# Moving the 16-bit low parts of the slot rows from GpSimd to VectorE in an early-fusion mixture-of-experts block

## What is computed

```python
h = patch_embed(x); h = concat([h, txt], axis=1)                 # 32 x 333 x 192
h = h + sdconv(layernorm(h))      # per token: softmax over 9 taps, weighted window of 9 values
xf = layernorm(h).reshape(-1, D)
scores, idx = top_k(xf @ Wg, 2); weights = softmax(scores)
for k in range(2):                # capacity int(1.2 * N / 8) tokens per expert and choice
    xg = xpad[buf]                # gather the tokens of each expert
    h1 = einsum('ecd,edh->ech', xg, W1)
    ye = einsum('ech,ehd->ecd', h1[..., :H] * silu(h1[..., H:]), W2)
    out = out.at[buf].add(w_buf * ye)
h = h + out
```

## Time and profile before

| what | value |
|---|---|
| median of 3 runs | 1479.6 us (1479.3 to 1480.26) |
| the profiled execution's own time | 1478.12 us |
| its span, first to last instruction | 1476.2 us |
| stage 1, up to the first matmul of stage 2 | 808.5 us |
| busy in the span: PE, DVE, ACT, POOL | 85%, 67%, 30%, 48% |

### The profile page before, as it was taken

How to read it: one execution, slowest core, us unless ns; L and a number is a source line. 1 busy time by engine, 2 the same in 40 slices (tenths; PEclk the granted TensorE clock), 3 DMA queues, 4 the chain that set the end, 5 groups by cost and what they waited for, 6 DMA issues and landing times. The chain is left out here.

```text
span 1476.2 us, 23362 instructions
## 1 busy us (share of the span) xinstructions
PE 1249.6 (85%) x8476; PEld 991.4 (67%) x8476; DVE 991.2 (67%) x1924; ACT 449.7 (30%) x949; POOL 715.1 (48%) x545
## 2 busy tenths in 40 slices
PE   6969888988989798843640999999999999999994
PEld 6757666777767576533330787787777778877873
DVE  4107959999999999997841565656564655656552
ACT  2011222223232222212031443434442434344331
POOL 1000221766666665746376345545556255455455
PEclk9989998999989898765755999999999999999997
DMA  9795563655656554623024455464656365554533
GB/s 328 299 357 154 134 175 87 183 150 158 180 161 171 153 139 110 155 74 100 23 69 122 84 79 89 62 111 55 103 61 106 58 100 64 91 78 61 71 46 36
DMA packets 224279, 178.52 MB, mean 121 GB/s; under 512 B 128872, under 2 KB 208006, under 8 KB 224160
## 3 DMA queue, kind: packets, MB, share of 16 engines
q1 hardware_dynamic: 176896, 117.16, 32.7%
q0 software_dynamic: 37248, 36.15, 16.1%
q10 hardware_dynamic: 10016, 23.66, 4.3%
HBM read 69.22 MB, written 89.23 MB: 107 GB/s over the span
## 5 line engine op out<-in xcount | busy, mean ns | idle before, releaser
L1127 POOL DMA_INDIRECT out<-yb,meta x200 | 329.4, 1647 | 323.2 <-DVE yb L1184 252.2
L1216 DVE TENSOR_TENSOR hidden<-silu,bankU 128x320 f32<-128x320 f32 x320 | 155.2, 487 | 198.0 <-PE bankU L1249 172.7
L902 PE MATMUL bankK<-normedT,conv_w 128*128 128x333 f32 x864 | 278.7, 471 | 0.0
L85 POOL DMA_INDIRECT expert_inputs<-slot_rows,slots x176 | 230.0, 1307 | 78.4 <-issue 55.0
L1156 ACT ACTIVATE silu<-bankG 128x320 f32<-128x320 f32 x320 | 139.8, 437 | 379.7 <-PE bankG L1249 358.4
L902 PEld LDWEIGHTS bankK<-normedT,conv_w 128*128 128x128 f32 x864 | 169.5, 202 | 78.0 <-issue 13.1
L1262 PE MATMUL bankY<-w_high,hidden_high 128*128 128x192 f16 x800 | 197.2, 246 | 0.0
L1263 PE MATMUL bankY<-w_low,hidden_high 128*128 128x192 f16 x800 | 197.2, 246 | 0.0
L1264 PE MATMUL bankY<-w_high,hidden_low 128*128 128x192 f16 x800 | 197.2, 246 | 0.0
L652 DVE TENSOR_TENSOR prod<-window_values,kb 128x960 f32<-128x960 f32 (+1 forms) x135 | 168.3, 1255 | 3.6
L670 DVE TENSOR_TENSOR hidden_group<-hidden_group,prod 128x960 f32<-128x960 f32 (+1 forms) x135 | 169.1, 1253 | 0.5
(11 more groups left out here) (131 smaller groups left out, 2212.7 us busy)
## 6 DMA issues: line engine op xcount, KB each, us to landing
patches<-in_x SPq DMA_DIRECT2D x16, 1536.0 KB, 8.6
token_rows<-rowbuf SPq DMA_DIRECT2D x32, 492.0 KB
expert_inputs<-prod ACTq DMA_DIRECT2D x8, 1470.0 KB, 15.0
window_values<-token_rows SPq DMA_DIRECT2D x32, 264.0 KB, 5.5
hidden_group<-token_rows SPq DMA_DIRECT2D x32, 264.0 KB, 7.1
expert_inputs<-prod ACTq DMA_DIRECT2D x8, 980.0 KB, 16.6
window_values<-token_rows SPq DMA_DIRECT2D x32, 192.0 KB, 5.7
kb<-token_rows SPq DMA_DIRECT2D x32, 148.5 KB, 4.7
```

The costliest lines, as they stand in the source:

```text
L85: nc.gpsimd.indirect_dma_start(out=xslots[:, :], out_offset=bass.IndirectOffsetOnAxis(ap=idx[g % 2][:, k, r:r + 1], axis=0), in_=xrow[g % ...
L902: mm = T_.matmul(bankK[(u + t) % 2][:, 0:L], conv_w[:, t // 2, k, :], qT[u][:, t, k:k + L], start=(k == 0), stop=(k == K - 1))
L1127: nc.gpsimd.indirect_dma_start(out=out[:, :], out_offset=bass.IndirectOffsetOnAxis(ap=meta[t % NMETA][:, c, 0:1], axis=0), in_=yb[v][:, c, ...
L1216: V.tensor_tensor(hf[j % 2][:, m * HALF:(m + 1) * HALF], sg[m][:, :], bankU[m][:, 0:HALF], ALU.mult).then_inc(prod_done, 1)
```

## The change

`low_parts` is also defined for DVE, with the same two subtractions (L682 and L683 in the changed kernel, for L375 and L376). DVE does the low parts of both slices of groups 0 to 5 and of slice 0 of group 6: 13 of 16 calls. Slice 1 of a group is done one iteration later than POOL did it, in front of slice 0 of the next group, right behind the norm of the iteration's second pair. Its last two calls, (5, 1) and (6, 0), stand behind the loop. POOL keeps (6, 1), (7, 0) and (7, 1), and its scatters now wait for DVE.

```diff
 # POOL
                 for it in range(NG):
                     pair_norm(2 * it + 1)
-                    if it > 1:
-                        low_parts(it - 2, 0)
                     if it > 2:
                         scatter(it - 3, 0)
...
                     if it > 2:
                         scatter(it - 3, 1)
-                    if it > 1:
-                        low_parts(it - 2, 1)
                     if it:
                         slice_norm(it - 1, 0)
-                low_parts(NG - 2, 0)
                 scatter(NG - 3, 0)
 # DVE
+                def low_parts(g, s):
+                    ss, x16 = slice(*SLICES[s]), xrow16[g % 2]
+                    dve.wait_ge(xh_ready, NSL * g + s + 1)
+                    V.tensor_tensor(x16[:, ss, LOB:LOA], xn[:, ss, 128:D], x16[:, ss, 128:D], ALU.subtract)
+                    V.tensor_tensor(x16[:, ss, LOA:META], xn[:, ss, 0:128], x16[:, ss, 0:128], ALU.subtract)\
+                        .then_inc(xl_ready, 1)
...
                     attend(p, 0)
                     if it:
                         norm(p + 1)
+                    if it > 2:
+                        low_parts(it - 3, 1)
                     if it > 1:
+                        low_parts(it - 2, 0)
                         part(2)
...
                 g, h = NG - 1, NG - 2
+                low_parts(NG - 3, 1)
+                low_parts(NG - 2, 0)
                 part(2 * NSL * K)
```

## The result

| what | before | changed |
|---|---|---|
| median, first comparison | 1479.45 us (4 runs) | 1490.07 us (4 runs, 1488.19 to 1491.62) |
| ratio to before | | 1.0065, 95% interval 1.0044 to 1.0085 |
| the same two kernels again (run z1) | 1478.92 us (17 runs) | 1492.32 us (6 runs), ratio 1.0089, 1.0072 to 1.0106 |
| profiled execution's own time | 1478.12 us | 1490.28 us |
| its span | 1476.2 us | 1488.5 us |

The change costs 10.6 us by the medians and 12.2 between the profiled executions; 8.2 were forecast. All but 0.2 of the 12.2 lies in stage 1, whose end came 12.0 later.

A forecast was written before the change was run, and what follows sets the result against it. DVE, busy 75.73 of 80.20 us an iteration, was taken as the bound. The terms 12.5 - 5.1 - 1.5 + 0.3 + 2.0 gave +8.2 us on 1479.6, so 1487.8 us, own range 1484.0 to 1492.4.

The forecast's parts named there:

- the first rival: The port between POOL and DVE stays contested, L636 stays long and 5.1 us come back: 1493 us, chance 0.15.
- Added to DVE: Iterations 3 to 7: four subtractions lengthen each by 2.5 us, +12.5 us in all, bounds +11.1 and +14.1.
- Clash removed: Iterations 3 to 7: without POOL's low parts (L375, L376), DVE's L636 falls back to 1.40 us, -5.1 us in all.
- A DMA wait covered: L632's wait for the window DMA in three iterations vanishes as DVE arrives 2.5 us later: -1.5 us, bound 0.
- The other waits: DVE's waits on the text DMA and PE start from L636 or later and move along: 0.
- Iteration 2: Only slice 0's subtractions, 1.35 us against 1.20 given back at L636: +0.3 us, between 0 and 0.8.
- The tail: Behind the loop: DVE waits 4.0 us for high parts, POOL's slice norm starts 1.1 later: +2.0 us, -0.1 to +3.0.
- The port stays contested: L636 stays long beside scatters, and DVE's subtractions can hold up POOL's pair norm: +13.3 us, 1493, chance 0.15.
- A wash: All low ends, and the tail costs nothing: +1 to +3 us, about 1481 us, chance 0.12.
- Faster: A loop over POOL, ACT and PE back to DVE sets the period; subtractions fill waits: 1471 us, chance 0.07.

The follow-up runs named there:

- z2: The changed kernel with each pair of DVE's subtractions done twice, the second time over the same data: 1510.43 us, 1.0207.
- y3: Kernel before, POOL's slice 0 low parts held until slice 1's windows are through, tail slice norm (6, 1) before low parts and scatters: 1485.63 us, 0.9995.
- x4: The changed kernel without the two subtractions in DVE's 13 calls, those low parts left zero, waits and semaphore raises kept: 1483.28 us, 0.9983.
- x3: The kernel before with POOL's low parts of slice 0 moved behind the first seven scatters, nothing moved to DVE: 1488.24 us, 1.0036.
- z4: The kernel before with only low parts (0, 0) of iteration 2 on DVE, all others on POOL: 1479.45 us, 1.0003.
- x1: The changed kernel with its two tail calls, (5, 1) and (6, 0), back on POOL as before: 1495.96 us, 1.0080.
- the filler: A quarter of PE's patch matmuls put ahead of the third set of transposes: changed kernel 1485.82 us, 1.0013; kernel before 1479.08 us, 0.9968.
- x2: The changed kernel with the loop's low parts on DVE moved from ahead of the softmax's top to behind attend(p, 2): 1498.4 us, 1.0088.
- y2: The kernel before with a quarter of PE's patch matmuls put ahead of the third set of transposes: 1479.08 us, 0.9968.
- z3: y2 with POOL's slice norm (6, 1) put ahead of its low parts and scatters in the tail: 1472.09 us, 0.9948.

## Why the prediction was right, and where its sum was short

The forecast, slower by about 8 us, was right in its sign and its main mechanism; 10.6 to 12.2 came in the first comparison and 13.4 in the second. The second ratio put on the forecast's base of 1479.6 gives 1492.8, at the far end of its own range (1492.4) and where the first rival stood, so the sum was short by more than it looks in the first comparison. Between the two traces (before to the changed kernel), by its own terms:

- **Added to DVE, +12.5.** 2.46 us a block, five of them 12.3. That more of it lengthens the loop one for one is shown by z2.
- **Clash removed, -5.1.** L631 is 1.40 everywhere, as forecast. But the credit is DVE time, and it counts only while DVE is the bound: y3 took the clash away alone and gained nothing (0.9995), and x4, without the work on any engine, gained nothing in iterations 3 to 6. In the changed kernel it pays for part of DVE's new work; the kernel before could not have had it as a gain.
- **A DMA wait covered, -1.5.** Gone from the list, as forecast.
- **The other waits, 0.** Here the sum was short by a little: the text DMA's wait rose by 2.4 us, the waits for PE fell by 1.7 (1.0 on the key bank, 0.7 on the value bank), and 0.2 on another DMA is new: +0.9. Iterations 3 to 7 thus cost 6.6 us where 12.5 - 5.1 - 1.5 = 5.9 had been put.
- **Iteration 2, +0.3, bound 0.8.** This is the term that was furthest off between the two traces: +3.8. The bound took in the pair norm on POOL behind DVE's subtractions, and that did happen, 1.3 us. What the bound left out is PE's clock: it is 0.79 and no longer 1.00 in the patches' stretch, and they take 1.7 us more; 0.7 and 0.4 more of waits on two DMAs follow. But not all of that is the change's. x3 has 1.7 us of lost clock in this iteration with the order of the kernel before, and y3 1.3; the trace of before, with none, is the fortunate one. Over all traces of both kinds the iteration is about 2.5 longer (z4): above the bound, by less than two executions differ. And z4's total shows no cost from this call alone, at most 2.8 us.
- **The tail, +2.0.** +1.9 between the traces, and x1 takes 2.3 off by undoing it. The new wait (3.31 for 4.0 forecast), the undisturbed windows and the shorter wait for the exponential (6.62 for 8.44) came. That the sum is right within 0.1 is luck: counted from DVE's arrival, POOL's norm started 0.5 later for 1.1 forecast, and took 4.1 us (695.86 to 699.99) for 3.6. The prediction's "3.6, the middle" is no middle of 2.0 and 4.6 either (3.3), and its lower bound should be 686.5 + 2.0 = 688.5 and not 688.1, which makes its low end of the sum +4.9.

These make 6.6 + 3.8 + 1.9 = 12.3; less 0.5, by which the changed kernel's trace was ahead at iteration 2, and with 0.2 more behind group 7's exponential, that is the 12.0 at the start of stage 2.

The rivals. *The port stays contested* did not come in the form that was priced, L636 staying long. Its second half, the subtractions holding up POOL's pair norm "on which ACT and PE wait", did in iteration 2 (3.9 us for 2.6 from the statistics to ACT's start). In iterations 3 to 7 it did not: it is 4.8 us there, for 4.0 to 5.2 before. Here the trace agrees with the rule of the Trainium skill (SBUF — State Buffer, Who interferes with whom) in both directions: L354 went from 1.32 to 1.92 us behind DVE, and DVE's L651 from 1.16 to 2.48 beside L376 in x3. *A wash*, with the warning of Perfetto Trace Analysis (Optimizing Scalar/DVE Operations) in the Trainium skill, is ruled out by both intervals: the work moved did not break even. *Faster* needed a loop that sets the period in DVE's place. x4 shows that such a bound is there, at 80.1 us, the length of the kernel before's iterations; it was no help since DVE came to lie above it, at 81.8 us in iterations 3 to 6.

What the sum had at nothing in iterations 3 to 6 is that PE is held up with DVE. The exponential starts 9.85 us after the statistics for 8.6 to 8.9 before, the patches 11.8 to 12.0 after them for 10.5 to 10.8, and they took 9.3 to 9.7 us in iterations 3 to 5, as they did in z1, whose iterations 3 to 6 are 3.8 us longer still. With the filler in both kernels the change costs 6.7 us and not 10.6 to 13.4, so some 4 to 7 us of its price go with PE's lateness (4 us would be within the intervals, 7 are clear of them). How much of that is the clock is not shown: the filler also takes PE's waits away by itself, and x2, with the patches at full clock in every iteration, has a loop as long as the changed kernel's.

## What to carry to other kernels

Before work goes from an idle engine to the bound engine, price its whole time on the bound one and take the clash it ends as credit only up to the second bound; an experiment that leaves the work out altogether shows where that bound is. Before a term is read off two traces, look at the same stretch in other runs with the same order there: iteration 2 differs by 2.7 us between such traces. Follow an engine that will start a microsecond late to what it does next. The gains here lay in order alone, with filler matmuls where PE waited (y2, 0.9968) and, on top, the norm ahead of the scatters in the tail (z3, 0.9948; its own part is seen in the trace and not yet in the totals).

## What the runs showed of the hardware

- **PE's clock behind a later start.** The same 48 matmuls took 8.01 us at a granted clock of 1.00 and 9.69 in a stretch at 0.79. In iterations 3 to 5 of the changed kernel's traces (first, z1, x1) they began 11.8 to 12.0 us after DVE's statistics and took 9.17 to 9.69 all nine times; in the kernels where they began 10.0 to 10.9 after them (before, x2, x3, x4, y3, z4) they took 8.01 every time. PE had stood idle for 2.1 to 2.2 us ahead of them in the first kind and for 0.5 to 2.0 in the second. It is no rule: in iteration 6 of the first trace and of x1, with the same start and the same idle time, they took 8.01.
- **The same program can lose its clock in one execution and not in another.** In iteration 2 the kernel before had its patches at 8.01 and the convolution behind them at 5.25; x3, with the same order there, had 8.01 and 6.95 (its granted clock from 208 to 216 us was 0.79, that of the kernel before 1.00); x2 had 8.01 and 6.84. In the changed kernel, x1, x4, z1 and z4 it was the patches that lost, 9.69, and the convolution stood at 5.25. What decides the place is left open.
- **A clash between POOL and DVE looks for its victim.** The same L376 took 1.64 us and cost L636 0.77 to 1.20 in one place, and took 2.55 and cost DVE's windows 2.0 to 2.1 in another (x3). The operation's place decides the price; where POOL was held back until the windows were through, in y3, none of DVE's two-input operations was lengthened in iterations 3 to 7 (L636 1.40, windows of 960 elements 1.15 to 1.16).
